# bf16 norm factors, f16 feed-forward, probabilities scaled ahead of their transposes, and values held in the array: one kernel of a causal block and six local blocks

## The reference

```python
# stage 1: modulated layer norm, causal attention with 16 heads of 64, residual (once)
# stage 2: DEPTH = 6 layers; each layer:
qkv = x @ Wqkv                                   # 128 -> 3 * 1024, 16 heads of 64
q = l2norm(q) * qs;  k = l2norm(k) * ksc
q = q*cos*scale + rotate_half(q)*sin*scale       # k likewise with 1/scale
sim = einsum('bhwie,bhwje->bhwij', bq, bk2) * 8  # windows of 32 queries, 64 keys (own and previous window)
out = einsum('bhwij,bhwje->bhwie', softmax(mask(sim)), bv2)
x = x + out @ Wo
xn = layernorm(x) * g + bln
a, gate = split(xn @ W1 + b1)                    # 128 -> 2 * 341
x = x + a * gelu(gate) @ W2 + b2                 # 341 -> 128
```

## Time and profile before

| what | value |
|---|---|
| timed runs | 3932.16, 3932.62, 3944.91 us |
| profiled execution | span 3944.5 us; the timed run that stands next to it took 3944.91 us |
| PE busy | 3691.1 us, 94% of the span |
| DVE busy | 2985.9 us, 76% |
| ACT busy | 2392.9 us, 61% |
| POOL busy | 2310.3 us, 59% |
| float32 matmuls | each shows as two records of PE |

### The profile page before, as it was taken

One profiled execution on the slowest core, in us unless ns is written; L12 is line 12 of the kernel. 1 busy time (PEld: TensorE's weight loads), 2 busy tenths in 40 slices (PEclk: granted clock), 3 DMA queues, 4 the chain that ended last, 5 costly groups with the idle time before them and its releaser, 6 DMA issues.

```text
span 3944.5 us, 165118 instructions
## 1 busy us (share of the span) xinstructions
PE 3691.1 (94%) x73780; PEld 2146.6 (54%) x73780; DVE 2985.9 (76%) x3451; ACT 2392.9 (61%) x2931; POOL 2310.3 (59%) x1892
## 2 busy tenths in 40 slices
PE   7999998799999999999999999999999999999996
PEld 4666665455555555555555455555555555555553
DVE  7888886677777777777777677777777777777774
ACT  6777776455656655566555565555565656666652
POOL 4555654666655666656666565656565655666651
PEclk9999999899999999999999999999999999999998
DMA  1000001444444444445354444444444444444442
GB/s 59 5 5 7 5 5 39 106 100 111 101 101 104 108 108 104 101 95 123 89 121 95 97 103 108 108 107 96 109 112 109 101 101 103 110 103 106 101 101 77
DMA packets 162073, 349.17 MB, mean 89 GB/s; under 512 B 32606, under 2 KB 41948, under 8 KB 155100
## 3 DMA queue, kind: packets, MB, share of 16 engines
q1 hardware_dynamic: 161372, 338.62, 37.4%
HBM read 24.54 MB, written 4.19 MB: 7 GB/s over the span
## 4 chain that ended last, share of the span: by engine, by line
PE 66%; issue 5%; DMA 4%; ACT 3%; SPq 2%; DVE 2%; POOL 1%; ACTq 0%; DVEq 0%; POOLq 0%
PE psB L677 32%; PE psA L677 26%; DMA vev<-vo 3%; PE psA L732 3%; PE psB L758 2%; PE psB L732 2%; ACT pb L1015 1%; PE psA L758 1%; ACT vo L1007 1%; SPq L502 1%; SPq L486 1%; SPq L504 1%; DMA kf<-h 1%; DVE h L1253 0%; ACT sq L985 0%
## 5 line engine op out<-in xcount | busy, mean ns | idle before, releaser
L1354 POOL TENSOR_TENSOR sq<-sq 128x512 f32<-128x512 f32 x384 | 490.1, 1295 | 492.6 <-ACT sq L985 492.3
L1349 POOL TENSOR_TENSOR h<-h,ts 128x512 f32<-128x512 f32 x384 | 490.3, 1277 | 211.1 <-DVE ts L1245 211.1
L1329 POOL TENSOR_TENSOR pt<-wk,pt 128x256 f16<-128x256 f32 (+3 forms) x256 | 368.0, 1453 | 286.6 <-ACT pt L908 196.9
L1350 POOL TENSOR_TENSOR h<-h,ts 128x512 f32<-128x512 f32 x384 | 489.6, 1275 | 0.0
L985 ACT ACTIVATE sq<-psA 128x1024 f32<-128x1024 f32 x240 | 245.7, 1024 | 168.3 <-PE psA L677 168.2
L1237 DVE TENSOR_TENSOR h<-psA,t_rot 128x1024 f32<-128x1024 f32 x240 | 293.0, 1221 | 38.1 <-ACT sq L985 17.3
L677 PE MATMUL psB<-vev,ptb 64*32 64x65 f32 x9216 | 244.4, 225 | 59.0 <-ACT pb L1015 35.2
L1245 DVE TENSOR_TENSOR ts<-psA,t_rot 128x1024 f32<-128x1024 f32 x240 | 291.6, 1215 | 3.1 <-POOL h L1350 3.1
L677 PEld LDWEIGHTS psB<-vev,ptb 64*32 64x32 f32 x9216 | 194.7, 106 | 175.5 <-issue 103.3
L1364 POOL TENSOR_SCALAR f_a<-f_a 128x512 f32<-128x512 f32 x48 | 31.2, 650 | 401.6 <-DVE f_a L1293 401.6
L1253 DVE TENSOR_TENSOR h<-h,psB 128x1024 f32<-128x1024 f32 x192 | 229.5, 1217 | 42.4 <-PE psB L677 40.3
(11 more groups left out here) (343 smaller groups left out, 10637.5 us busy)
## 6 DMA issues: line engine op xcount, KB each, us to landing
qf<-h SPq DMA_DIRECT2D x768, 136.0 KB, 2.5
kf<-h SPq DMA_DIRECT2D x768, 136.0 KB
vev<-vo SPq DMA_DIRECT2D x192, 260.0 KB, 4.1
vev<-vo SPq DMA_DIRECT2D x192, 227.5 KB, 4.6
stage<-wqk SPq DMA_DIRECT2D x12, 512.0 KB, 4.6
stage<-wvl SPq DMA_DIRECT2D x12, 256.0 KB, 5.3
stage<-wof SPq DMA_DIRECT2D x6, 512.0 KB, 5.1
xb<-xt SPq DMA_DIRECT2D x8, 256.0 KB, 8.1
```

The lines of the kernel that those rows point to most:

```text
L1329: e.tensor_tensor(pt[g][pr][:, :, 1, o:o + w], wk[(slot_of(s)[0] - 1) % SLOTS][:, :, 0:w], pt[g][pr][:, :, 0, o:o + w], ALU.subtract).then ...
L1349: e.tensor_tensor(halves_of(h, 0), halves_of(h, 0), t[1], ALU.subtract)
L1350: e.tensor_tensor(halves_of(h, 1), halves_of(h, 1), t[0], ALU.add).then_inc(ended["ad"])
L1354: e.tensor_tensor(sqb[c][:, 0, :], sqb[c][:, 0, :], sqb[c][:, 1, :], ALU.add).then_inc(ended["qa"])
```

## The change

- **Norm factors in bf16.** After `nw`, `n_a` is cut into three bf16 parts by rows: `ca` (ACT) copies it to bf16 where a mask `less` allows, `cs` (POOL) subtracts, `cb` (ACT) copies again, `ct` (POOL) subtracts into `n_b` (bf16). `bc` multiplies `n_b` by a bf16 `spread` that adds up the parts: the same 2 matmuls a step, now bf16.
- **Feed-forward in f16 pairs.** `fh` (ACT) and `fl` (POOL) split `f_c`; `gh` (ACT) and `gl` (POOL), three each, split the gated values. The weights are split once a layer on DVE (`first_halves`, `second_halves`) into `w1s` and `w2s`, scaled by `WF = 8`. `f` is 3 steps of 6 f16 matmuls, `fo` 9 f16 matmuls. The bias b2 is a row of W2. `feed_of` runs at half-step 8 of the layer before.
- **Probabilities normalized ahead of transposing.** `sm` (DVE) sums `pb` over keys and takes reciprocals; `pn` (POOL) multiplies all of `pb` (128x1024 float32) by them, in place. `pb` has two buffers. `nm` and its reciprocals are gone.
- **Values held in the array.** In `pv` the stationary operand is the 64x64 values and the moving one 64x32 of `ptb`. The output comes with features in partitions, so `ot` is gone, `oe` and `ol` read the tile of `pv`, and one PSUM tile takes both steps `pv` of a head pair (before: one each, and one for `ot`). The column of ones in `vo` and `vev` is gone.
- **Orders.** All five texts are new.

```diff
-                    for tq in range(2):
-                        for x in range(2):
-                            for g in range(4):
-                                t = 2 * th + tq
-                                vals = vo[v % 2] if g % 2 else vev
-                                for q in range(2):
-                                    at = 512 * q + 65 * (2 * tq + x)
-                                    rows = slice(64 * q, 64 * q + 64)
-                                    p = mm(o[32 * g:32 * g + 32, at:at + 65], ptb[rows, x, t, 32 * g:32 * g + 32],
-                                           vals[rows, 2 * t + g // 2, 2 * rp + x, :], tile_position=(64 * q, 32 * g))
+                    for tq in range(2):
+                        for g in range(4):
+                            t = 2 * th + tq
+                            vals = vo[v % 2] if g % 2 else vev
+                            for x in range(2):
+                                for q in range(2):
+                                    rows, at = slice(64 * q, 64 * q + 64), 512 * q + 128 * t + 32 * g
+                                    p = mm(o[64 * x:64 * x + 64, at:at + 32], vals[rows, 2 * t + g // 2, 2 * rp + x, :],
+                                           ptb[rows, x, t, 32 * g:32 * g + 32], tile_position=(64 * q, 64 * x))
...
-                        p = mm(o[:, 512 * x:512 * x + 512], spread[rows, :], n_a[rows, :], tile_position=(64 * k + 32 * x, 0))
+                        p = mm(o[:, 512 * x:512 * x + 512], spread[rows, :], n_b[rows, :], tile_position=(64 * k + 32 * x, 0))
...
-                        p = mm(o[0:n, 512 * x:512 * x + 512], w1r[:, FF * x + 128 * j:FF * x + 128 * j + n], f_c[:, :])
+                        mm(oy, w1s[1][:, at:at + n], f_ch[:, :], True, False)
+                        mm(oy, w1s[0][:, at:at + n], f_cl[:, :], False, False)
+                        p = mm(oy, w1s[0][:, at:at + n], f_ch[:, :], False, True)
...
-                        p = mm(o[:, 0:512], w2r[0:n, j, :], f_g[j][0:n, :], j == 0, j == 2)
+                        mm(o[:, 0:512], w2s[1][0:n, j, :], f_gh[j][0:n, :], j == 0, False)
+                        mm(o[:, 0:512], w2s[0][0:n, j, :], f_gl[j][0:n, :], False, False)
+                        p = mm(o[:, 0:512], w2s[0][0:n, j, :], f_gh[j][0:n, :], False, j == 2)
...
+                elif kind == "sm":
+                    e.wait_ge(*done("ex", v, rp))
+                    e.tensor_reduce(sums[rp][:, :], pbs[rp].rearrange("p x t (f s) -> p (x t f) s", f=2), AXX, ALU.add).then_inc(s_rc)
+                    e.wait_ge(s_rc, count[s])
+                    e.reciprocal(rc[rp][:, :], sums[rp][:, :]).then_inc(ended["sm"])
...
+                elif kind == "pn":
+                    w = pbs[rp].rearrange("p x t (f s) -> p (x t f) s", f=2)
+                    e.wait_ge(*done("sm", v, rp))
+                    e.tensor_tensor(w, w, rc[rp][:, :].unsqueeze(2).to_broadcast([128, 16, 2 * W]), ALU.mult).then_inc(ended["pn"])
...
+                elif kind == "ca":
+                    e.activation(n_c[:, :], n_a[:, :], ACT.Copy, scale=less[:, 0:1]).then_inc(ended["ca"])
+                elif kind == "cs":
+                    e.tensor_tensor(n_a[:, :], n_a[:, :], n_c[:, :], ALU.subtract).then_inc(ended["cs"])
+                elif kind == "cb":
+                    e.activation(n_c[:, :], n_a[:, :], ACT.Copy, scale=less[:, 1:2]).then_inc(ended["cb"])
+                elif kind == "ct":
+                    e.tensor_tensor(n_b[:, :], n_a[:, :], n_c[:, :], ALU.subtract).then_inc(ended["ct"])
+                elif kind == "fh":
+                    e.activation(f_ch[:, :], f_c[:, :], ACT.Copy).then_inc(ended["fh"])
+                elif kind == "fl":
+                    e.tensor_tensor(f_cl[:, :], f_c[:, :], f_ch[:, :], ALU.subtract).then_inc(ended["fl"])
+                elif kind == "gh":
+                    e.activation(f_gh[j][0:n, :], f_g[j][0:n, :], ACT.Copy).then_inc(ended["gh"])
+                elif kind == "gl":
+                    e.tensor_tensor(f_gl[j][0:n, :], f_g[j][0:n, :], f_gh[j][0:n, :], ALU.subtract).then_inc(ended["gl"])
...
 VECTOR = (
+    "fm0 bm12 bm13 tc01+1 ts01+1 fm2 tc03+1 ol10 ts03+1 tc02+1 wl1 ts02+1 ol11 fm1 mx00+1 tc10+1 ts10+1 sm00+1 mx01+1 "
+    "rs bm00+1 bm01+1 sm01+1 bm02+1 bm03+1 ln+1 tc11+1 ol00+1 ts11+1 tc13+1 ts13+1 tc12+1 wl0+1 mx10+1 ts12+1 sm10+1 "
+    "ol01+1 tc00+2 mx11+1 ts00+2 fr ow bm10+1 bm11+1 sm11+1 "
 GPSIMD = (
-    "lx qa10 ad10 qa11 qa13 qa12 ad11 xl+1 ad13 nw1 ad12 qa01+1 ad01+1 ad00+1 qa00+1 qa03+1 qa02+1 ad03+1 nw0+1 "
-    "ad02+1 "
+    "gl1 cs0+1 pn00+1 ct0+1 ad10+1 qa10+1 qa11+1 pn01+1 lx+1 qa13+1 qa12+1 ad11+1 ad13+1 nw1+1 qa00+2 cs1+1 fl+1 "
+    "ct1+1 pn10+1 ad12+1 pn11+1 ad00+2 xl+2 qa01+2 ad01+2 qa03+2 qa02+2 gl0+1 ad03+2 gl2+1 ad02+2 nw0+2 "
```

More of the change, by code:

```diff
@@ L24 @@
 FP = [128, 128, FF - 256]
+FK = [128, 128, FF - 255]
 NEG = -1e30
@@ L27 @@
 WS = 64.0
+WF = 8.0
 TINY = WS * WS * 1e-24
@@ L203, in walk, with with_first @@
     return out, rings
+def with_first(steps, *first):
+    return list(first) + [s for s in steps if s not in first]
 def ordinals(walks):
@@ L326, in program @@
         f_g = [sb(f"f_g{j}", [128, S]) for j in range(3)]
+        f_ch, f_cl = (sb("f_c" + z, [128, S], F16) for z in "hl")
+        f_gh, f_gl = ([sb(f"f_g{z}{j}", [128, S], F16) for j in range(3)] for z in "hl")
+        w1s = [sb("w1" + z, [128, 2 * FF], F16) for z in "hl"]
+        w2s = [sb("w2" + z, [128, 3, 128], F16) for z in "hl"]
+        t_gs = sb("t_gs", [128, L])
         x1d = nc.dram_tensor("x1_keep", [NB, 128, S], F32).ap()
@@ L342, in program @@
         s_wa = sems("s_wa", 3)
-        s_const, s_first, s_ct, s_x, s_wo, s_wm, s_w1, s_w2, s_tab, s_stage, s_x1r = (
-            sem("s_" + n) for n in ("const", "first", "ct", "x", "wo", "wm", "w1", "w2", "tab", "stage", "x1r"))
+        s_const, s_first, s_cin, s_x, s_wo, s_wm, s_w1, s_w2, s_tab, s_stage, s_x1r = (
+            sem("s_" + n) for n in ("const", "first", "cin", "x", "wo", "wm", "w1", "w2", "tab", "stage", "x1r"))
         s_dm = sems("s_dm", 4)
@@ L508, in sync @@
                     heads_of(e, li + 1, 0)
-                if u == 2 and li:
-                    e.wait_ge(*all_done("f", *((NB * li - 1, j) for j in range(3))))
-                    e.wait_ge(*done("fo", NB * li - 1))
-                    feed_of(e, li)
+                if u == 8 and li + 1 < L:
+                    e.wait_ge(*done("lb", NB * li))
+                    e.wait_ge(s_w1s, li + 1)
+                    e.wait_ge(s_w2s, li + 1)
+                    feed_of(e, li + 1)
             e.wait_ge(*done("ss", 2 * NB * L - 1))
@@ L1038, in local_scalar @@
                     if v:
-                        e.wait_ge(*all_done("f", *((v - 1, j) for j in range(3))))
+                        e.wait_ge(*done("fl", v - 1))
                     e.wait_ge(*done("la", v))
@@ L1206, in weights_low, with first_halves, second_halves @@
                                    ).then_inc(ended["wl"])
+        def first_halves(e, li):
+            e.wait_ge(s_w1, 16 * (li + 1))
+            g = t_gs[:, li:li + 1]
+            e.tensor_scalar(w1s[0][:, :], w1r[:, :], g, None, ALU.mult).then_inc(s_w1h)
+            e.wait_ge(s_w1h, li + 1)
+            e.scalar_tensor_tensor(out=w1s[1][:, :], in0=w1r[:, :], scalar=g, in1=w1s[0][:, :], op0=ALU.mult,
+                                   op1=ALU.subtract).then_inc(s_w1s)
+        def second_halves(e, li):
+            e.wait_ge(s_w2, 48 * (li + 1))
+            for j in range(3):
+                n = FK[j]
+                e.tensor_scalar(w2s[0][0:n, j, :], w2r[0:n, j, :], WF, None, ALU.mult).then_inc(s_w2h)
+            e.wait_ge(s_w2h, 3 * li + 3)
+            for j in range(3):
+                n = FK[j]
+                p = e.scalar_tensor_tensor(out=w2s[1][0:n, j, :], in0=w2r[0:n, j, :], scalar=WF, in1=w2s[0][0:n, j, :],
+                                           op0=ALU.mult, op1=ALU.subtract)
+            p.then_inc(s_w2s)
         def local_vector(e):
@@ L1212, in local_vector @@
                 e.memset(t[:, :, S // 2:S // 2 + W], 0.0)
-            for n in range(2):
-                e.memset(vo[n].rearrange("p c r d -> p (c r) d")[:, :, 64:65], 1.0)
             e.memset(vev.rearrange("p c r d -> p (c r d)"), 0.0).then_inc(s_init)
+            e.memset(f_gh[2][64:128, :], WF).then_inc(s_ones)
+            e.memset(f_gl[2][64:128, :], 0.0).then_inc(s_ones)
+            e.tensor_scalar(t_gs[:, :], t_vec[:, V_LAYER:V_LAYER + 10 * L].rearrange("p (l c) -> p l c", c=10)[:, :, 0], WF, None,
+                            ALU.mult).then_inc(s_ones)
+            e.wait_ge(s_ones, 3)
+            first_halves(e, 0)
+            second_halves(e, 0)
             for s in vector_walk[1:]:
@@ L1302, in local_vector @@
                                            in1=f_g[j][0:n, :], op0=ALU.add, op1=ALU.mult).then_inc(ended["fm"])
+                    li = v // NB + 1
```

(2 more changed lines are left out.)

194 lines of the change are left out of this document (100 added, 94 removed), and 16 rows, old and new, of tables (SCALAR, TENSOR, VECTOR).

## The result

The changed kernel takes 3761.76 us (median of 4 runs, 3755.88 to 3769.58), the kernel before 3932.39 us beside it (4 runs): ratio 0.9558, 95% interval 0.9537 to 0.9579, 171 us less. The forecast was 3768 us. The size came out, the explanation only in part: a half-step got shorter than forecast, the layer changes got longer, and the bound is not the one that was named.

What follows compares the result with a forecast made beforehand. PE was taken to bound the kernel before, POOL the changed one: 29.3 us at 95% fill makes 30.9 a half-step, 1.7 less. Over 96 half-steps 165 us come off, giving 3768 us, range 3690 to 3885.

Steps and rivals of the forecast that it cites:

- PE bounds the kernel before: Stage 2 before the change: PE, busy 96.4% with 31.43 us of work a 32.6 us half-step, sets the pace.
- PE's sum, 26.8 us a half-step: PE's work after the change: 31.43 - 2.16 - 1.65 - 1.33 + 0.5 = 26.8 us, ends 24.5 and 30.4.
- rival 1: PE stays the bound by its loads: `pv` doubles to 7.08 us, `bc` runs one after another; 3828 us, chance 0.12.
- `pn` at 2.44 us: POOL's multiplication of the probabilities, 1024 columns, takes 2.44 us; two a half-step are 4.9 us.
- rival 2: `pn` on POOL is slow in its shape, 4.3 us: +211 us, 4143 us; chance 0.08.
- POOL's sum, 29.3: POOL's work a half-step: 19.85 + 4.6 + 4.9 = 29.3 us, range 28.7 to 29.6.
- The bound moves to POOL, filled to 95%, 30.9 us: Half-step: POOL's 29.3 us exceed PE's 26.8; at 95% fill 30.9 us, 1.7 less than before.
- Chains hidden: Norm chain grows 3.6 us, probabilities' 3.9; DVE's 13.6 us of slack a unit hides its stand of some 6 us.
- rival 3: POOL, DVE and ACT wait on each other, POOL fills only to 90%: 32.6 us a half-step, 3933 us; chance 0.10.
- rival 4: Clock falls to 0.87 in PE's new idle time, PE's 26.8 us become 30.8: 3885 us; chance 0.08.
- Layer changes stay as they are: The five layer changes keep their length; splitting the weights on DVE may be 3 us a layer, within its slack.
- The sum: Whole kernel: 96 x 1.7 = 165 us off the profiled execution, 3780 us, 3768 us for the median of runs.

Runs made afterwards that it cites:

- experiment 2: Changed kernel without the matmuls of the low halves `f_cl` and `f_gl` on PE; ratio 0.9568 to the kernel before, +4 us against the changed kernel.
- Experiment 12: Changed kernel with every matmul of `pv` made as two of 16 moving columns each; ratio 1.1273 to the kernel before.
- experiment 4: Changed kernel with `pn` multiplying by a full second operand instead of the repeated factor; ratio 0.9564 to the kernel before, `pn` 1896 ns.
- experiment 1: Changed kernel with POOL's three `gl` subtractions cut to one column each; ratio 0.9517 to the kernel before, -16 us against the changed kernel.
- experiment 8: Changed kernel with the norm in one bfloat16 piece, without `ca`, `cs`, `cb`, `ct`; ratio 0.9508 to the kernel before, -20 us.
- experiment 3: Changed kernel with `gl` cut to one column and the `f_cl` and `f_gl` matmuls left out; ratio 0.9532 to the kernel before, -10 us.
- Experiment 9: Changed kernel with `gl` cut, `f_cl` and `f_gl` matmuls and the norms' second and third bfloat16 pieces left out; ratio 0.9464 to the kernel before, -37 us.
- experiment 6: Changed kernel without splitting the feed-forward weights after the first layer; ratio 0.9466 to the kernel before, -36 us, 7 a change.

## Why the prediction was right, and where it was not

- *PE bounds the kernel before*: not tested, since no run took work away from that kernel. For it speaks that the unit fell by 6.2 us as PE's busy time fell by 6.6. Against it: in the changed kernel PE is at 95.0%, hardly less than the 96.1% of the window above, and there experiment 2 gained nothing. In `bc` and `pv` of the changed kernel added work of PE comes out in full.
- *PE's sum, 26.8 us a half-step*: 168.17 / 6 = 28.0. `bc` was right (0.60 forecast, 0.71 measured). `f` and `fo` saved about 1.0 a half-step where 1.33 was forecast. Their matmuls start every 0.217 us, as in the earlier trace rows, but the 18 of `f` come in three groups of six, and each group's last record (0.38 us) runs out by itself: 1.47 us a group, not 1.30. `pv` was forecast at 4.0 and is 4.56: the largest mis-sized term of PE.
- *Why `pv` was mis-sized*: the forecast took it that neither side of the matmul sets its price, since 32 loads start within 0.18 us. That is the opening burst of a step. Over the window a record took 13.8 ns, which is loads of 0.11 us eight deep, not twenty. In the changed kernel they start eight in 0.12 us all the way:
```profile
1010.45 0.21 PEld L673 LDWEIGHTS psB<-ptb,vo 64*64 64x64 f32 x8
...
1011.15 0.21 PEld L673 LDWEIGHTS psB<-ptb,vo 64*64 64x64 f32 x8
```
  Experiment 12 excludes the moving columns. Left are the 64 stationary columns that are loaded, the four tiles in use instead of eight, and the start of each matmul; no run parts these. The Trainium skill ("TensorE: Matmul & The Clock Gate", LDWEIGHTS) has a load cost its columns over 1.2 GHz, an estimate of 53 ns here; with 17.8 ns a record three would overlap. The record did move the way that this rule points, from 13.8 to 17.8 ns, but did not double as rival 1 had it.
- *`pn` at 2.44 us*: 1.905. It was worked out from an f16 result at 2154 ns plus twice a difference of formats; that step failed. With it rival 2 (the slow shape) is refuted, and experiment 4 shows that the repeated factor makes no difference.
- *POOL's sum, 29.3*: 168.10 / 6 = 28.0; `pn` accounts for 1.1 of the 1.3. *DVE 24.1, ACT 22.1*: 23.7 and 21.6.
- *The bound moves to POOL, filled to 95%, 30.9 us*: the fill is 95.0% and the half-step 29.5, but the step "so the bound moves to POOL" failed. With `pn` at its real price the forecast's own rule, 28.0 / 0.95, gives just the 29.5 measured; that fit is luck. Taking 1.4 us a half-step from POOL (experiment 1), or 2.0 (experiment 8), moved an ordinary unit by at most 0.1 us. POOL is full at the pace that something else sets; stretches of its order lie on the chain. That PE kept 95%, not 87, was the sign. DVE's waits at `mx` did come as forecast; those at `bm` are not among its longest.
- *Chains hidden* (rival 3): the chain of the norm could be shortened without effect, so its lengthening was hidden, as forecast. Yet something other than an engine's fill holds the unit at 58.4 to 59.1 us in experiments 3, 8 and 9, with PE at 92% in 3 and 9. A circuit over the orders is what is left; no run shows it as a whole.
- *The clock* (rival 4): inside a layer it is 1.00 in 17 of 18 ordinary units. Around the changes it is lower than before: 20 of the first 46 units are below 1.00, where 11 were.
- *Layer changes stay as they are*: failed, by 14 us a change. Half of it is the splitting of weights on DVE (experiment 6, 7 us), which was priced at no more than 3 us a layer. Beside an idle POOL that is right: 0.58 + 0.93 + 0.49 + 0.69 = 2.7 us for the first layer. What the forecast had at nothing is POOL beside it: one change has 3.09 + 0.93 + 4.11 + 0.69 = 8.8 us. The tables are 4 us of a change, but they were made there before as well. The rest goes with the lower clock, and what comes first there is open.
- *The sum*: about 270 us off at the ordinary pace instead of 165, less what five changes and both ends gave back. Two errors of opposite sign met, and 3768 is nearer to 3762 than the steps deserved.

What stays open: which links close the circuit of 58.4 us. That there is one is argued, by excluding the rest. The runs exclude as its sole link the pieces of the norms, the low parts of the feed-forward and the ring of `h`, and they show `bc` and `pv` of PE to lie on it. No run changed an order, which would be the direct test. How the other 93 us divide between holding the values, the feed-forward, the normalizing and the new orders was not taken apart. Experiment 9 is faster than the changed kernel, but it leaves out low parts that the precision needs; no run that keeps them was measurably faster.
